# A fused embedding, interaction and MLP kernel: the Gram steps of a group in pairs, and another order for the last group

## The chip, the cores and the metric

The kernel runs on one core of a Trainium2 chip. The metric is the time of one execution on the device in microseconds. A core has five engines with queues of their own: TensorE (PE in the profile; its weight loads are shown apart as PEld), VectorE (DVE), ScalarE (ACT), GpSimd (POOL) and SyncE (SP), which here only issues DMAs. They wait for one another by semaphores.

## What is computed

A recommendation model's forward pass, for a batch of 2048 samples, in fp32:

```
e_k = tbl_k[ids[:, k]]                      # 26 tables, rows of 128
c   = [dense, e_0, ..., e_25]               # 27 features of 128 for each sample
z   = c_n . c_m for all n < m               # 351 products for each sample
h   = relu([dense, z, dense] @ W_top1 + b_top1)   # 607 -> 512
h   = relu(h @ W_top2 + b_top2)                   # 512 -> 256
y   = h @ W_top3                                  # 256 -> 1
```

## The kernel before

The batch is cut into 8 groups of 256 samples, and a group into 2 tiles of 128. Each group goes through these stages.

- **Looks.** Ten tables have only 1000 rows. They stay in SBUF, split into a high and a low part (`table_high`, `table_low`). VectorE compares ids with row numbers (`matches`, L455) and TensorE multiplies the tables by these 0/1 matrices: `look(g, r)` (L300) is 16 matmuls of 256 columns. ScalarE copies the result, transposed, into the tile `turned` (`take_look`, L498). There are two `match` buffers, so the match of a look may be written once the look two before it has ended.
- **Gathers and turns.** The other 16 tables are gathered by POOL with indirect DMAs, 128 rows each, four tables at a time (L284 to L293). `turn(g, k)` (L315) transposes four such blocks on TensorE, 4 matmuls. A group has 8 turns: turns 0 to 3 for its first tile, 4 to 7 for its second. `take_turned` (L504) copies each into `turned`.
- **Gram steps.** `gram(g, k)` (L325) multiplies, for a quarter of the group's samples, the 27 features of each by themselves. In the profile one step is 128 small matmuls (32 columns of weights, 27 moving), each with a weight load of its own. A group has 4 steps. `take_gram` (L516) copies a step's result into the tile `grams`.
- **Repack.** SP writes `grams` to a scratch buffer in HBM and reads it back into `pairs`, in the layout that layer 1 wants (`repack`, L209). It waits for the copy of the last Gram step.
- **Layers.** `layer1(g, o)` (L344) for o = 0 to 3 is 8 matmuls each, `layer2` (L361) 16, `layer3` (L369) 4; ScalarE applies bias and relu (`relu1`, `relu2`) and copies y.

Turns and Gram steps share three PSUM buffers, `mid_ps`. They are numbered in the order in which TensorE issues them (`turn_number`, L168; `gram_number`, L176); an item uses buffer number % 3 and waits until the item three before it has been copied out:

```
after(pe, mid_out, number - 2)
```

The order of all this is written out by hand, once for TensorE (L376 to L451) and once, to match, for ScalarE (L543 to L620). In the period of group g (L391 on), TensorE runs the Gram steps of group g-1, turns of group g, looks of groups g and g+1, and the layers of group g-2:

```
gram(g-1,0) turn(g,0) look(g,6) layer1(g-2,0) layer1(g-2,1)
gram(g-1,1) turn(g,1) look(g,7) layer1(g-2,2) layer1(g-2,3)
gram(g-1,2) turn(g,2) look(g,8) layer2(g-2)
gram(g-1,3) turn(g,3) look(g,9) layer3(g-2)
turn(g,4) look(g+1,0) look(g+1,1) turn(g,5) look(g+1,2)
turn(g,6) look(g+1,3) turn(g,7) look(g+1,4) look(g+1,5)
```

The last group has an order of its own (L428 to L451), in which its own four Gram steps follow too, before the layers of the groups 6 and 7. SP's queue is also in a fixed order (L255 to L271): ids for later looks, the repack, the store of y.

Of the kernel before, what the change touches and what calls it, by code (L numbers as in the profile page):

```python
# [15 lines left out]
AHEAD = 6  # L16
# [6 lines left out]
TURNS = TILES * UNITS  # L23
# [20 lines left out]
def build(nc, dense_t, index_t, look_rows_t, tables, w1_dense, w1_pairs, b1, w2, b2, w3, y):  # L44
# [11 lines left out]
    with ctx:  # L56
# [104 lines left out]
            return 2 * number + 2  # L161

        PERIOD = TURNS + STEPS

        def turn_number(g, k):  # L168
            if g == 0:
                return k  # L170
            first = TURNS + PERIOD * (g - 1)
            if k >= STEPS and g + 1 == groups:
                return first + (10, 11, 12, 13)[k - STEPS]
            return first + (2 * k + 1 if k < STEPS else k + STEPS)

        def gram_number(g, k):  # L176
            first = TURNS + PERIOD * g
            if g + 1 == groups:
                return first - PERIOD + (8, 9, 14, 15)[k]
            return first + 2 * k  # L180

        block = ctx.enter_context(nc.Block())

# [115 lines left out]
        def _(pe):  # L299
            def look(g, r):  # L300
                number, pair = look_number(g, r), pair_number(g, r // 2)
                if g == 0:
                    pe.wait_ge(tables_split, r + 1)

                after(pe, looked, pair - 1)
                pe.wait_ge(match_ready, number + 1)
                for c in range(PARTS):
                    for part in (table_high, table_low):
                        last = nc.tensor.matmul(look_ps[pair % 2][:, r % 2, :], part[0:table_rows, r, c, :],  # L309
                                                match[number % 2][0:table_rows, c, :],  # L310
                                                start=(c == 0 and part is table_high),
                                                stop=(c == PARTS - 1 and part is table_low))
                last.then_inc(look_done, 1)

            def turn(g, k):  # L315
                j, u = g * TILES + k // UNITS, k % UNITS
                number = turn_number(g, k)
                after(pe, mid_out, number - 2)
                pe.wait_ge(gathered[j % 2][u], 16 * UNIT_OF * (j // 2 + 1))
                for n in range(UNIT_OF):  # L320
                    last = nc.tensor.transpose(mid_ps[number % 3][:, n * P:(n + 1) * P],  # L321
                                               rows[j % 2][:, u * UNIT_OF + n, :], identity[:])
                last.then_inc(turn_done, 1)

            def gram(g, k):  # L325
                number = gram_number(g, k)
                if k == 0:

                    pe.wait_ge(mid_out, turn_number(g, TURNS - 1 if g + 1 < groups else UNITS - 1) + 1)
                    pe.wait_ge(looked, pair_number(g, LOOK_PAIRS - 1) + 1)  # L330
                    pe.wait_ge(dense_put, g + 1)
                if k == STEPS // TILES and g + 1 == groups:
                    pe.wait_ge(mid_out, turn_number(g, TURNS - 1) + 1)
                after(pe, mid_out, number - 2)
                for i in range(IN_STEP):
                    for s in range(QUADS):
                        x = k * IN_STEP + i
                        n = (x // BLOCK * P + s * BLOCK + x % BLOCK) * FEATURES
                        last = nc.tensor.matmul(  # L339
                            mid_ps[number % 3][s * ROW:(s + 1) * ROW, i * FEATURES:(i + 1) * FEATURES],  # L340
                            turned[g % 2][:, n:n + ROW], turned[g % 2][:, n:n + FEATURES], start=True, stop=True)
                last.then_inc(gram_done, 1)
# [18 lines left out]
            def layer2(g):  # L361
                pe.wait_ge(hidden1_ready, L1 * (g + 1))
                for o in range(L2):
                    for c in range(L1):
                        last = nc.tensor.matmul(layer_ps[0][:, o, :], w2_sb[:, c, o * P:(o + 1) * P], hidden1[:, c, :],  # L365
                                                start=(c == 0), stop=(c == L1 - 1))
                last.then_inc(layer2_done, 1)

            def layer3(g):  # L369
                pe.wait_ge(hidden2_ready, L2 * (g + 1))  # L370
                for c in range(L2):
                    last = nc.tensor.matmul(layer_ps[1][0:1, 0, :], w3_sb[:, c:c + 1], hidden2[:, c, :],  # L372
                                            start=(c == 0), stop=(c == L2 - 1))
                last.then_inc(layer3_done, 1)
# [16 lines left out]
            for g in range(1, groups - 1):  # L391
                if g == 2:
                    pe.wait_ge(weights_summed, 1)
                    pe.wait_ge(weights_in, WEIGHT_DMAS)
                gram(g - 1, 0)
                turn(g, 0)
                look(g, 6)
                if g >= 2:
                    layer1(g - 2, 0)
                    layer1(g - 2, 1)  # L400
                gram(g - 1, 1)
                turn(g, 1)
                look(g, 7)
                if g >= 2:
                    layer1(g - 2, 2)
                    layer1(g - 2, 3)
                gram(g - 1, 2)
                turn(g, 2)
                look(g, 8)
                if g >= 2:  # L410
                    layer2(g - 2)
                gram(g - 1, 3)
                turn(g, 3)
                look(g, 9)
                if g >= 2:
                    layer3(g - 2)
                turn(g, 4)
                look(g + 1, 0)
                look(g + 1, 1)
                turn(g, 5)  # L420
                look(g + 1, 2)
                turn(g, 6)
                look(g + 1, 3)
                turn(g, 7)
                look(g + 1, 4)
                look(g + 1, 5)

            g = groups - 1  # L428
            for k in range(STEPS):
                gram(g - 1, k)  # L430
                turn(g, k)
                look(g, AHEAD + k)
            layer1(g - 2, 0)
            layer1(g - 2, 1)
            gram(g, 0)
            layer1(g - 2, 2)
            gram(g, 1)
            turn(g, 4)
            turn(g, 5)
            turn(g, 6)  # L440
            turn(g, 7)
            layer1(g - 2, 3)
            gram(g, 2)
            layer2(g - 2)
            gram(g, 3)
            layer3(g - 2)
            for g in (groups - 2, groups - 1):
                for o in range(L1):
                    layer1(g, o)
# [42 lines left out]
        def _(act):  # L492
# [71 lines left out]
            act.wait_ge(weights_in, WEIGHT_DMAS)  # L564
            for g in range(1, groups - 1):
                take_gram(g - 1, 0)
                take_turned(g, 0)
                if g >= 2:
                    relu1(g - 2, 0)
                take_gram(g - 1, 1)  # L570
                take_turned(g, 1)
                take_look(g, 3)
                if g >= 2:
                    relu1(g - 2, 1)
                take_gram(g - 1, 2)
                take_turned(g, 2)
                if g >= 2:
                    relu2(g - 2)
                take_gram(g - 1, 3)
                take_turned(g, 3)  # L580
                take_look(g, 4)
                if g >= 2:
                    copy_y(g - 2)
                take_turned(g, 4)
                take_look(g + 1, 0)
                take_turned(g, 5)
                put_dense(g)
                take_turned(g, 6)
                take_look(g + 1, 1)
                take_turned(g, 7)  # L590
                take_look(g + 1, 2)
            g = groups - 1
            take_gram(g - 1, 0)
            take_turned(g, 0)
            take_gram(g - 1, 1)
            take_turned(g, 1)
            take_look(g, 3)
            take_gram(g - 1, 2)
            take_turned(g, 2)
            put_dense(g)  # L600
            take_gram(g - 1, 3)
            take_turned(g, 3)
            take_look(g, 4)
            relu1(g - 2, 0)
            take_gram(g, 0)
            take_gram(g, 1)
            take_turned(g, 4)
            take_turned(g, 5)
            take_turned(g, 6)
            take_turned(g, 7)  # L610
            relu1(g - 2, 1)
            take_gram(g, 2)
            relu2(g - 2)
            take_gram(g, 3)
            copy_y(g - 2)
            for g in (groups - 2, groups - 1):
                for half in range(2):
                    relu1(g, half)
# [51 lines left out]
```

## Time and profile before

| | us |
|---|---|
| median of 3 runs | 382.88 (381.33 to 383.34) |
| the profiled execution | 384.91 |
| its span, first to last instruction | 382.8 |
| PE busy, matmuls | 341.9 (89%) |
| PE busy, weight loads | 304.2 (79%) |
| POOL busy | 252.1 (66%) |
| DVE busy | 193.2 (50%) |
| ACT busy | 125.5 (33%) |

The profile shows one execution. Matmuls overlap, so a matmul's duration is longer than its share of the time; the distance from one start to the next tells what it costs. "Idle before" is the time for which an engine did nothing in front of an instruction, and "<-" names what ended it; "issue" stands where the profile shows nothing that was waited for. The mean clock granted to TensorE was 0.991 of 2.4 GHz.

### The profile page before, as it was taken

The numbers are of one execution on the slowest core, as the hardware profiler recorded it, in microseconds if no ns is written. First come the engines' busy times: TensorE is split into PE (matmuls) and PEld (weight loads), VectorE is DVE, ScalarE is ACT, GpSimd is POOL, SyncE is SP. The second block draws the span as 40 slices with busy tenths as digits, with TensorE's granted clock in tenths as the row PEclk, the third lists the DMA queues.
The fourth block names the chain that finished last, engine by engine and source line by source line (L and its number), as shares of the span: only waits on it lengthen the run. The fifth ranks groups of instructions, "written<-read, shape, count | busy, mean of one in ns | idle before, by whom it ended". The sixth has DMA issues, their size and how long they took to land.

```text
span 382.8 us, 13108 instructions
## 1 busy us (share of the span) xinstructions
PE 341.9 (89%) x6048; PEld 304.2 (79%) x6048; DVE 193.2 (50%) x94; ACT 125.5 (33%) x211; POOL 252.1 (66%) x267
## 2 busy tenths in 40 slices
PE   0788878984999999999999999999999999999995
PEld 0687767883898898898988898889988898977763
DVE  2899996565424396228833495238742595100000
ACT  2235433332132341334322342323322333343122
POOL 3777887777777777777777777777777777500200
PEclk9999999999799999999999999999999999999999
DMA  8975698254322537225632536234622533420400
GB/s 205 222 210 166 170 301 250 58 195 126 126 80 58 193 82 200 58 80 177 149 119 58 194 92 190 58 120 140 187 79 58 193 89 86 144 73 27 154 13 0
DMA packets 30868, 49.57 MB, mean 129 GB/s; under 512 B 17499, under 2 KB 17635, under 8 KB 30686
## 3 DMA queue, kind: packets, MB, share of 16 engines
q1 hardware_dynamic: 22350, 31.68, 27.0%
q0 software_dynamic: 8320, 16.92, 16.8%
q8 instruction: 48, 0.79, 0.9%
q10 hardware_dynamic: 144, 0.13, 0.1%
q14 instruction: 6, 0.05, 0.0%
HBM read 38.21 MB, written 10.49 MB: 127 GB/s over the span
## 4 chain that ended last, share of the span: by engine, by line
PE 72%; POOL 14%; issue 6%; DMA 4%; DVE 2%; ACT 1%; DVEq 0%
PE look_ps L309 28%; POOL rows L290 14%; PE mid_ps L339 13%; PE layer_ps L356 11%; PE layer_ps L365 7%; PE mid_ps L321 7%; PE layer_ps L353 4%; DMA rows<-in_table,index 3%; DVE match L463 2%; PE layer_ps L372 2%; DMA index<-in_index 1%; ACT hidden L528 0%; ACT hidden L534 0%; ACT turned L501 0%; ACT turned L512 0%
## 5 line engine op out<-in xcount | busy, mean ns | idle before, releaser
L290 POOL DMA_INDIRECT rows<-in_table,index x256 | 248.8, 972 | 82.3 <-issue 75.0
L463 DVE TENSOR_TENSOR match<-look_ids,row_number_ps 125x2048 fp32r<-125x2048 int32 x80 | 181.7, 2286 | 132.2 <-PE look_ps L309 122.3
L309 PE MATMUL look_ps<-match,table_high 125*128 125x256 f32 x640 | 165.7, 296 | 20.2 <-DVE table_low L471 18.1
L309 PE MATMUL look_ps<-match,table_low 125*128 125x256 f32 x640 | 159.4, 286 | 0.1
L309 PEld LDWEIGHTS look_ps<-match,table_high 125*128 125x128 f32 x640 | 124.8, 195 | 25.0 <-issue 16.0
L309 PEld LDWEIGHTS look_ps<-match,table_low 125*128 125x128 f32 x640 | 125.1, 195 | 0.0
L339 PEld LDWEIGHTS mid_ps<-turned 128*32 128x32 f32 x4096 | 45.3, 109 | 19.1 <-issue 15.3
L339 PE MATMUL mid_ps<-turned 128*32 128x27 f32 x4096 | 54.4, 195 | 5.5 <-issue 1.7
L501 ACT COPY turned<-look_ps 128x512 f32<-128x512 f32 x40 | 31.9, 798 | 73.5 <-PE look_ps L309 72.2
L508 ACT COPY turned<-mid_ps 128x512 f32<-128x512 f32 x64 | 42.8, 672 | 19.7 <-PE mid_ps L321 19.5
L321 PE MATMUL mid_ps<-identity,rows 128*128 128x128 f32 x256 | 40.6, 283 | 9.4 <-DMA rows<-in_table,index 8.5
L356 PE MATMUL layer_ps<-pairs,w_pairs_sb 117*128 117x256 f32 x192 | 46.7, 378 | 0.0
L356 PEld LDWEIGHTS layer_ps<-pairs,w_pairs_sb 117*128 117x128 f32 x192 | 36.3, 189 | 5.2
L321 PEld LDWEIGHTS mid_ps<-identity,rows 128*128 128x128 f32 x256 | 28.4, 142 | 14.0 <-issue 13.0
L521 ACT COPY grams<-mid_ps 128x432 f32<-128x432 f32 x32 | 16.6, 519 | 49.2 <-PE mid_ps L339 49.2
L365 PE MATMUL layer_ps<-hidden,w_sb 128*128 128x256 f32 x128 | 29.3, 381 | 1.9 <-ACT hidden L528 1.9
L528 ACT ACTIVATE hidden<-layer_ps,b_sb 128x256 f32<-128x256 f32 x32 | 13.4, 470 | 51.3 <-PE layer_ps L356 51.3
L365 PEld LDWEIGHTS layer_ps<-hidden,w_sb 128*128 128x128 f32 x128 | 23.7, 190 | 5.6 <-ACT hidden L528 2.7
L189 POOL DMA_DIRECT2D pairs<-scratch x4 | 2.5, 639 | 26.7 <-DMA scratch<-grams 26.7
L353 PE MATMUL layer_ps<-dense,w_dense_sum 128*128 128x256 f32 x64 | 19.4, 384 | 0.0
L534 ACT ACTIVATE hidden<-layer_ps,b_sb 128x256 f32<-128x256 f32 x16 | 6.7, 470 | 33.6 <-PE layer_ps L365 33.6
L353 PEld LDWEIGHTS layer_ps<-dense,w_dense_sum 128*128 128x128 f32 x64 | 11.1, 191 | 1.8 <-issue 0.4
(21 smaller groups left out, 44.8 us busy)
## 6 DMA issues: line engine op xcount, KB each, us to landing
look_ids<-in_look_rows SPq DMA_DIRECT2D x40, 256.0 KB, 4.4
scratch<-grams SPq DMA_DIRECT2D x8, 864.0 KB, 4.4
rows<-in_table,index POOLq DMA_INDIRECT x256
scratch<-grams SPq DMA_DIRECT2D x8, 416.0 KB, 5.2
pairs<-scratch SPq DMA_DIRECT2D x92, 29.2 KB
grams<-in_table SPq DMA_DIRECT2D x4, 448.0 KB
pairs<-in_table SPq DMA_DIRECT2D x3, 448.0 KB
hidden<-in_table SPq DMA_DIRECT2D x3, 448.0 KB
```

The costliest lines, as they stand in the source:

```text
L290: pool.indirect_dma_start(out=rows[j % 2][:, at, :], out_offset=None, in_=tables[GATHERED[at]], in_offset=bass.IndirectOffsetOnAxis(ap=ind ...
L309: last = nc.tensor.matmul(look_ps[pair % 2][:, r % 2, :], part[0:table_rows, r, c, :], match[number % 2][0:table_rows, c, :], start=(c == ...
L321: last = nc.tensor.transpose(mid_ps[number % 3][:, n * P:(n + 1) * P], rows[j % 2][:, u * UNIT_OF + n, :], identity[:])
L339: last = nc.tensor.matmul(mid_ps[number % 3][s * ROW:(s + 1) * ROW, i * FEATURES:(i + 1) * FEATURES], turned[g % 2][:, n:n + ROW], turned[ ...
L353: nc.tensor.matmul(layer_ps[o // 2][:, o % 2, :], w1_dense_sum[:, o * P:(o + 1) * P], dense[:, g * N:(g + 1) * N], start=True, stop=False)
L356: last = nc.tensor.matmul(layer_ps[o // 2][:, o % 2, :], w1_pairs_sb[0:CHUNK_ROWS, c, o * P:(o + 1) * P], pairs[0:CHUNK_ROWS, g % 2, c, :] ...
L365: last = nc.tensor.matmul(layer_ps[0][:, o, :], w2_sb[:, c, o * P:(o + 1) * P], hidden1[:, c, :], start=(c == 0), stop=(c == L1 - 1))
L463: nc.vector.tensor_tensor(match[number % 2][0:table_rows], look_ids[b][0:table_rows, r % 2].unsqueeze(1).broadcast_to(shape), row_number_p ...
L501: nc.scalar.copy(by_sample[g % 2][:, :, 1 + 2 * pair:3 + 2 * pair], look_ps[number % 2][:].rearrange("d f n -> d n f")).then_inc(looked, 1)
L508: nc.scalar.copy(by_sample[g % 2][:, tile * P:(tile + 1) * P, first:first + UNIT_OF], mid_ps[turn_number(g, k) % 3][:].rearrange("d (f x) ...
L521: nc.scalar.copy(grams[:, :, k * IN_STEP:(k + 1) * IN_STEP], mid_ps[gram_number(g, k) % 3][:, 0:IN_STEP * FEATURES].rearrange("p (x j) -> ...
L528: nc.scalar.activation(hidden1[:, o, :], layer_ps[half][:, o % 2, :], ACT.Relu, bias=b1_sb[:, o:o + 1]).then_inc(hidden1_ready, 1)
```

## The change

In the period of each group, the Gram steps 0 and 1 of the group before stand together in front of turn 0, and the steps 2 and 3 together behind the second half of layer 1. In the last group the same pairs are made, with turns and looks two by two between them; behind them come all four parts of layer 1 of group 5, then the last group's steps 0 and 1 as a pair, layer 2 of group 5, the turns 4 to 7, layer 3, and the steps 2 and 3 as a pair. ScalarE's order follows. The numbers of turns and Gram steps, which give the PSUM buffer and the count to wait for, are now taken from a generator that lists them in the order of issue. No instruction of the computation is added or removed.

```diff
-        PERIOD = TURNS + STEPS
+        def mid_order():
+            yield from (("turn", 0, k) for k in range(TURNS))
+            for g in range(1, groups):
+                for k in (0, 2):
+                    yield from (("gram", g - 1, k), ("gram", g - 1, k + 1), ("turn", g, k), ("turn", g, k + 1))
+                if g + 1 < groups:
+                    yield from (("turn", g, k) for k in range(STEPS, TURNS))
+
+            yield from (("gram", g, 0), ("gram", g, 1))
+            yield from (("turn", g, k) for k in range(STEPS, TURNS))
+            yield from (("gram", g, 2), ("gram", g, 3))
+
+        mid_place = {step: number for number, step in enumerate(mid_order())}
...
@@ TensorE, groups 1 to 6
                 gram(g - 1, 0)
+                gram(g - 1, 1)
                 turn(g, 0)
                 look(g, 6)
                 if g >= 2:
                     layer1(g - 2, 0)
                     layer1(g - 2, 1)
-                gram(g - 1, 1)
                 turn(g, 1)
                 look(g, 7)
                 if g >= 2:
                     layer1(g - 2, 2)
                     layer1(g - 2, 3)
                 gram(g - 1, 2)
+                gram(g - 1, 3)
                 turn(g, 2)
                 look(g, 8)
                 if g >= 2:
                     layer2(g - 2)
-                gram(g - 1, 3)
                 turn(g, 3)
@@ TensorE, group 7
-            for k in range(STEPS):
+            for k in (0, 2):
                 gram(g - 1, k)
+                gram(g - 1, k + 1)
                 turn(g, k)
                 look(g, AHEAD + k)
+                turn(g, k + 1)
+                look(g, AHEAD + k + 1)
             layer1(g - 2, 0)
             layer1(g - 2, 1)
+            layer1(g - 2, 2)
+            layer1(g - 2, 3)
             gram(g, 0)
-            layer1(g - 2, 2)
             gram(g, 1)
-            turn(g, 4)
-            turn(g, 5)
-            turn(g, 6)
-            turn(g, 7)
-            layer1(g - 2, 3)
+            layer2(g - 2)
+            for k in range(STEPS, TURNS):
+                turn(g, k)
+            layer3(g - 2)
             gram(g, 2)
-            layer2(g - 2)
             gram(g, 3)
-            layer3(g - 2)
```

## Rows read from the trace of the kernel before

**Rows 1.** The page, busy time of each engine.
```profile
PE 341.9 (89%) x6048; PEld 304.2 (79%) x6048; DVE 193.2 (50%) x94; ACT 125.5 (33%) x211; POOL 252.1 (66%) x267
```

**Rows 2.** All waits: engine, tile and line, releaser, us in total, times, longest.
```profile
PEld mid_ps L339 <- issue: 15.3, 53, 1.8
```

**Rows 3.** Timeline of PE: start us, us, what, count, idle before.
```profile
96.35 1.09 PE L321 MATMUL mid_ps<-identity,rows 128*128 128x128 f32 x4 [4.26 <-DMA rows<-in_table,index]
```

**Rows 4.** Table of stretches: length, busy time (instructions), granted clock, DMA share, GB/s.
```profile
187.57:229.93 42.36, 41.68 (x758) 37.42 (x757) 22.68 (x11) 14.20 (x25) 32.00 (x35) 1.00 0.44 126
```

**Rows 5.** Table of stretches, L339 alone: Gram steps, start to the next operation's start.
```profile
195.32:197.21 1.89, 1.73 (x128) 1.00 0.22 54
210.83:212.33 1.50, 1.44 (x128) 1.00 0.24 63
336.41:337.63 1.22, 1.22 (x128) 1.00 0.05 13
...
sum 7.96, PE 7.04; mean PE 1.76
```

**Rows 6.** The page, DMA queues: packets, MB, share of 16 engines.
```profile
q8 instruction: 48, 0.79, 0.9%
```

**Rows 7.** Timeline of PE, last group.
```profile
314.99 1.72 PE L339 MATMUL mid_ps<-turned 128*32 128x27 f32 x116
317.00 0.32 PE L339 MATMUL mid_ps<-turned 128*32 128x27 f32 x12 [0.30 <-issue]
...
319.75 1.25 PE L339 MATMUL mid_ps<-turned 128*32 128x27 f32 x95
321.20 0.47 PE L339 MATMUL mid_ps<-turned 128*32 128x27 f32 x33 [0.20 <-issue]
...
324.10 1.06 PE L339 MATMUL mid_ps<-turned 128*32 128x27 f32 x74
325.40 0.90 PE L339 MATMUL mid_ps<-turned 128*32 128x27 f32 x54 [0.24 <-issue]
...
339.56 1.73 PE L339 MATMUL mid_ps<-turned 128*32 128x27 f32 x128
...
342.74 1.31 PE L321 MATMUL mid_ps<-identity,rows 128*128 128x128 f32 x10 [0.65 <-issue]
...
347.35 0.38 PE L339 MATMUL mid_ps<-turned 128*32 128x27 f32 x20 [0.30 <-issue]
```

**Rows 8.** DMA queues: the stretches 314.7 to 315.7, 318.5 to 319.9, 192.8 to 194.
```profile
q8 instruction: 1, 0.02, 5.5%
...
q8 instruction: 1, 0.02, 5.7%
...
q8 instruction: 1, 0.02, 4.6%
```

**Rows 9.** Table of stretches, all engines, as rows 4.
```profile
189.00:193.00 4.00, 4.00 (x73) 3.83 (x61) 1.93 (x2) 1.09 (x2) 2.91 (x4) 1.00 0.97 279
```

**Rows 10.** Timeline of PE, from a look into a Gram step.
```profile
187.24 0.28 PE L309 MATMUL look_ps<-match,table_high 125*128 125x256 f32 x1
187.36 0.28 PE L309 MATMUL look_ps<-match,table_low 125*128 125x256 f32 x1
187.57 0.62 PE L339 MATMUL mid_ps<-turned 128*32 128x27 f32 x49
```

**Rows 11.** Table of stretches, PE: a turn behind a Gram step, one behind a look.
```profile
189.35:189.77 0.42, 0.42 (x11) 1.00 0.82 307
180.52:180.88 0.36, 0.36 (x6) 1.00 0.09 22
```

**Rows 12.** Timeline of ACT, the last three copies of turned rows.
```profile
343.22 1.74 ACT L508 COPY turned<-mid_ps 128x512 f32<-128x512 f32 x3 [0.65 <-PE mid_ps L321]
```

**Rows 13.** Timeline of SP, the last repack's reads.
```profile
358.87 6.26 SPq L189 DMA_DIRECT2D pairs<-scratch  x8
```

**Rows 14.** Table of stretches, all engines, behind the wait of rows 3.
```profile
96.30:101.00 4.70, 4.65 (x22) 4.68 (x23) 0.04 (x1) 0.67 (x1) 3.48 (x5) 0.50 0.46 149
```

More of the change, by code:

```diff
@@ L161, in pair_end @@
             return 2 * number + 2
-        PERIOD = TURNS + STEPS
-        def turn_number(g, k):
[L169 to L174, printed above, removed]
+        def mid_order():
[9 more added lines that the diff above has]
+        mid_place = {step: number for number, step in enumerate(mid_order())}
+        def turn_number(g, k):
+            return mid_place["turn", g, k]
         def gram_number(g, k):
[L177 to L180, printed above, removed]
+            return mid_place["gram", g, k]
         block = ctx.enter_context(nc.Block())
@@ L566, in _ @@
                 take_gram(g - 1, 0)
+                take_gram(g - 1, 1)
                 take_turned(g, 0)
@@ L569, in _ @@
                     relu1(g - 2, 0)
-                take_gram(g - 1, 1)
                 take_turned(g, 1)
@@ L575, in _ @@
                 take_gram(g - 1, 2)
+                take_gram(g - 1, 3)
                 take_turned(g, 2)
@@ L578, in _ @@
                     relu2(g - 2)
-                take_gram(g - 1, 3)
                 take_turned(g, 3)
@@ L593, in _ @@
             take_gram(g - 1, 0)
+            take_gram(g - 1, 1)
             take_turned(g, 0)
-            take_gram(g - 1, 1)
             take_turned(g, 1)
@@ L598, in _ @@
             take_gram(g - 1, 2)
+            take_gram(g - 1, 3)
             take_turned(g, 2)
             put_dense(g)
-            take_gram(g - 1, 3)
             take_turned(g, 3)
@@ L604, in _ @@
             relu1(g - 2, 0)
+            relu1(g - 2, 1)
             take_gram(g, 0)
             take_gram(g, 1)
[L607 to L611, printed above, removed]
+            relu2(g - 2)
+            for k in range(STEPS, TURNS):
+                take_turned(g, k)
+            copy_y(g - 2)
             take_gram(g, 2)
-            relu2(g - 2)
             take_gram(g, 3)
-            copy_y(g - 2)
             for g in (groups - 2, groups - 1):
```

## The prediction, made before the changed kernel was run

> **What bounds the kernel now.** I read the page's engine table first: TensorE is busy 341.9 of 382.8 us, the next engine (POOL) 252.1 [rows 1]. Then the waits, of which the weight loads of the Gram steps hold 15.3 us with no engine named, only "issue" [rows 2]. PE's long idle stretches are in the opening; the last, 4.26 us for gathered rows, ends at 96.35, when the last block of rows of group 1 lands [rows 3]. Up to there the gathers set the pace. From 102.92 on, one group follows another, five of them alike; the one shown takes 42.36 us with PE busy for 41.68, in 758 matmuls [rows 4]. VectorE works 22.7 and ScalarE 14.2 us of it, so what is added to or taken from PE's own stream between 103 us and the end moves the end one for one. The change reorders that stream, so the question is what an order costs PE.
>
> **A limit that busy shares hide: PE's instruction supply.** A Gram step is 128 matmuls and 128 weight loads in 1.50 to 1.89 us [rows 5], while a look has 16 of each in 2.0 us. The table of queues has a queue "instruction" with 48 packets and 0.79 MB, 16.4 KB each [rows 6]; PE has 2 x 6048 instructions [rows 1] and some waits, 12,288 being 48 x 256. So PE's program comes in blocks of 256. Now read the pauses "<-issue" in the last group [rows 7]: the first Gram step pauses after 116 matmuls, the next after 95, the next after 74. From pause to pause that is 12 + 4 (a turn) + 16 (a look) + 95 = 127, and 33 + 4 + 16 + 74 = 127 matmuls: 254 instructions and two waits, 256 each time. Go on counting and you reach the middle of turn 5 (pause at 342.74) and matmul 108 of a later Gram step (pause at 347.35), both there in the rows. PE stops at borders of blocks.
>
> How fast can blocks follow? The block's packet lies in 314.7 to 315.7 and PE goes on at 317.00; in 318.5 to 319.9 and it goes on at 321.20 [rows 7, 8]. So the packet of the next block starts only after the border before it has been passed (317.00, then a packet after 318.5), one block is on its way at a time, and it is usable some 1.4 us after its packet. From border to border, where PE had to wait for it: 4.20 us twice, 4.6 (342.74 to 347.35), and 3.1 (the border 7 matmuls into the step at 339.56, to 342.74) [rows 7]. I call this turnaround R and take R = 4.0, bounds 3.1 and 4.6. Where other transfers are heavy it can be worse: after the border some 1.5 us into the step of 187.57, the packet is found only in 192.8 to 194 [rows 8], with the DMA engines 97% busy before it [rows 9]. That makes 192.9 + 0.9 + 1.4 - 189.1 = 6.1 us, which hurts nobody today, since 256 slow instructions follow.
>
> This is why order matters. At 1.75 us per 256 instructions a Gram step eats a block in less than half of R. Today each step is followed by 40 to 72 slow instructions, and the border in the next step is mostly reached after R is over.
>
> **The change, part by part.**
> *Steps 0 and 1 together (groups 2 to 6).* A period has 4 x 256 + 10 x 32 + 8 x 8 + 64 + 32 + 8 = 1512 instructions and about 20 waits, 1532 = 6 x 256 - 4: the borders wander by 4 instructions per group. In the last group the first lies 232 into the first step [rows 7], so in groups 2 to 6 it lies 212 to 228 into it. With one step after the other, the second border is 256 Gram instructions later, always inside the pair. It is due after 1.75 us and open after R: PE stands 4.0 - 1.75 = 2.25 us. Bounds: 1.35 (R 3.1), 4.35 (R 6.1; the ids' transfers that fill the DMA engines there are partly gated by the matches, so they stay near).
> *Steps 2 and 3 together.* The pair starts 664 instructions after the first one, so its borders lie at 60 to 76 and 316 to 332. Layer 1 in front is slow (108 ns per instruction, 3.46 us for 32) and lets instructions be queued ahead; I assume the first border is passed about 0.4 us before the pair starts. DMA is quiet around today's steps 1 and 3 (22 and 24% against 97% [rows 5, 9]), so R = 3.6: open at 3.2, due at 322 / 256 x 1.75 = 2.2, cost 1.0. Bounds 0.5 and 2.0 (R 3.1 and 4.6).
> *What goes.* Two entries and two exits of Gram steps per group. A step begins 0.21 us after a look's last matmul, where the next look matmul comes after 0.12 [rows 10], and a turn behind a step takes 0.42 us where it takes 0.36 behind a look [rows 11]; that is 0.15 a step, 0.3 per group.
> Of this the Trainium skill (TensorEngine Tiling (Array Packing), Key Properties) says that changing the tiling mode drains TensorE; the trace agrees, with 0.15 us as the drain's size. Such a rule alone would have this change win.
> Group: 2.25 + 1.0 - 0.3 = 2.95, five groups: 14.8 us.
> *Last group's first four steps.* Between the pairs stand two turns and two looks; the borders are at 228 and 484, then at 144 and 400 of the second pair: twice 2.25. Today the four slots from 314.99 on take 7.96 us, each from its step's start to the next turn's [rows 5], against 4 x 1.75: 1.0 us of waiting is paid already. 4.5 - 1.0 - 0.3 = 3.2.
> *The tail.* Steps 0 and 1 of group 7 have borders at about -3, 253 and 509, steps 2 and 3 at about 175 and 431: twice 2.25 again. What goes is today's wait in turn 5 (0.9 from start to start) and in step 2 (0.5), and 0.3 of entries. Added is a wait for ScalarE: after layer 2 of group 5 come its two relus (some 0.9 us), then four copies of turned rows (three take 1.74 us [rows 12], so 2.3 in all), while PE has the turns (1.7 us) and layer 3 (1.0) for cover in place of 1.8 us of layer 1: 3.2 against 2.7, about 0.5. Sum: 4.5 - 1.4 - 0.3 + 0.5 = 3.3. The last repack stays about hidden: the issues of its pairs run from 358.87 to 365.1 [rows 13], and the last layer 1 begins at some 367 today; layer 3 (0.7 us) no longer stands in that cover, so up to 0.5 more could show, which I keep for the range.
> *At nothing.* Group 1: its pairs cost 3 us too, but PE idles 4.26 us for rows behind them [rows 3], which absorbs it. It could even give something back: after the 4.26 us the granted clock is 0.50 for 4.7 us [rows 14], the lower level, 1.2 GHz; were the idle shorter, up to 2 us come back (not in the sum). ScalarE has the same operations; its copies are due later. Waits on the three turning buffers: each is for an item three back, and the item before a pair's turn is a turn or step that was copied at least a look earlier. SP's queue: the repack waits for step 3, which now stands one turn, one look and layer 2 earlier, hence scratch, pairs and ids move forward together. POOL's gathers wait for turns that come a little later; they run ahead by then.
>
> Sum: 14.8 + 3.2 + 3.3 = 21.3 us on the profiled execution's 384.91 us, 406.2. That execution is 2.0 us above the median of 382.88 (0.5%), so as a median: **404.2 us**.
>
> **Rivals.**
> A, *the supply keeps up* (381, faster): if two blocks or more were kept ahead, the pairs would cost nothing and only 0.3 us for each of seven stretches go: -2.1, with 0.5 back for the tail, so 381.3. It decides at the pair's second border: stall or none. For it: the weight loads of the steps pause 53 times, but 15.3 us in all [rows 2], and in groups 2 to 6 PE is nearly never idle. Against it: the 256 count and the constant lag behind the packet.
> The Trainium skill (Runtime: NRT & Kernel Launch, Instruction fetch mechanics) gives TensorE room for 2048 instructions, and by that a pair of 512 would never stall and rival A would hold; the same section also speaks of only two lines of 256. The trace sides with the second: 4.2 us per block when blocked.
> B, *even* (383): the short pauses inside steps, about 0.5 us of each slot (1.50 to 1.89 against 1.22 for the step at 336.41 [rows 5]), are not repeated in a pair's second step and pay for much of the stall. It needs R below 2.3, under every interval read.
> C, *the clock falls too* (432): idle of 2 us in 14 pairs lowers the granted clock as it did after 4.26 us; each time 4.7 us at half clock would cost about 2 us: 28 more. Against it: pauses of 0.65 us (0.9 from start to start) are followed by none that the table of slots shows [rows 5], and 2.2 us is nearer to these than to 4.26.
>
> **Numbers.** Forecast 0.80, A 0.10, B 0.05, C 0.05. All terms at their low bounds: 1.55 x 5 + 1.4 + 1.0 = 10.2, with 2 back from the clock 8.2, 391; all high: 6.05 x 5 + 5.9 + 4.5 = 40.6, 423.5. The terms will not all sit at one end, so 391 to 416 leaves out A, B, C and the far end. About 0.5% can be told from no change: faster 0.09, same 0.06, slower 0.85.
>
> **What would show it.** Groups of about 45.3 us in place of 42.4. Gram pairs of 5.5 to 6 us (first) and 4.3 to 5 (second), with one pause "<-issue" of 1 to 2.5 us in each, 256 instructions after another border and 1.4 us behind an instruction packet. The opening to 96.35 unchanged. I am wrong if pairs take 3.5 us and the pauses don't grow; half wrong if the second pair shows none.

## The result, and the profile after

| | before | changed |
|---|---|---|
| median of 5 runs, us | 382.88 (380.83 to 383.71) | 426.52 (420.87 to 427.94) |
| ratio | | 1.110, 95% interval 1.103 to 1.117 |
| profiled execution, us | 384.91 | 420.87 |
| its span, us | 382.8 | 418.8 |
| granted clock, mean | 0.991 | 0.950 |

The changed kernel is 11% slower. The forecast was slower, 404.2 us, with a range that ended at 416. The ratio leaves out the two slowest runs of the changed kernel (427.26 and 427.94 us), which are over 1.5% above its fastest. The profiled execution is the fastest of the five; in the others the mean granted clock was 0.943 to 0.955, and the 5.6 us between it and the median have no trace of their own.

First the page of the changed kernel, busy times and the queue of instruction blocks. PE's busy time grew by 10 us, its span by 36; the blocks are the same 48.

```profile
PE 351.9 (84%) x6048; PEld 316.5 (76%) x6048; DVE 193.2 (46%) x94; ACT 126.2 (30%) x211; POOL 252.9 (60%) x267
...
q8 instruction: 48, 0.79, 0.8%
```

Then the waits of the changed kernel (engine, tile, line <- releaser: us in total, times, longest). The weight loads of the Gram steps [rows 2] went from 15.3 to 40.9 us of "issue" in the same 53 pauses, and the matmuls now show 29.8 us of their own. (These two overlap; the step's line is L341 here.)

```profile
PEld mid_ps L341 <- issue: 40.9, 53, 3.4
...
PE mid_ps L341 <- issue: 29.8, 19, 3.3
...
PEld mid_ps L341 <- ACT turned L511: 0.5, 1, 0.5
```

The last line is the wait for ScalarE in front of the last pair, which the prediction put at about 0.5 us.

The table of stretches for the groups 2 to 6, for the last group up to layer 1 of group 6, and for the rest (columns as in rows 4). What took 42.36 us [rows 4] takes 46.8 to 50.1, and the granted clock is no longer 1.00.

```profile
102.51:149.33 46.82, 43.47 (x758) 39.24 (x757) 23.05 (x11) 14.41 (x25) 35.54 (x38) 0.96 0.43 117
149.33:197.36 48.03, 43.22 (x757) 38.92 (x757) 22.69 (x11) 14.28 (x25) 36.14 (x40) 0.96 0.42 117
...
292.65:342.73 50.08, 42.79 (x758) 39.09 (x757) 22.68 (x11) 14.40 (x25) 30.28 (x33) 0.93 0.34 91
342.73:387.98 45.25, 35.99 (x1174) 31.77 (x1173) 6.95 (x4) 14.38 (x26) 6.49 (x7) 0.95 0.17 52
387.98:418.80 30.82, 25.11 (x109) 19.32 (x104) 0.00 (x0) 6.28 (x15) 2.49 (x4) 0.94 0.16 55
```

The same table for the pairs of the groups 2 to 6 alone (columns as in rows 5; three of ten and the sum). The ten pairs take 55.3 us; the twenty steps of before sum up to 34.7, the second fence.

```profile
102.51:107.31 4.80, 3.41 (x256) 1.00 0.38 82
119.08:124.38 5.30, 3.65 (x256) 1.00 0.23 56
...
292.65:301.27 8.62, 3.58 (x256) 0.84 0.42 105
...
sum 55.32, PE 33.63; mean PE 3.36
```

```profile
sum 34.74, PE 32.71; mean PE 1.64
```

So the 36 us of the span go as follows. Groups 2 to 6: 240.2 - 212.1 = 28.2, of which 20.6 inside the pairs and 7.6 outside them. Last group up to layer 1 of group 6: 45.25 against 38.35 (314.99 to 353.34), 6.9. The rest 1.3, the opening -0.4.

The pauses stand where instructions were counted to. This is the timeline of PE in the changed kernel: both pairs of group 6, one of group 7.

```profile
292.65 1.58 PE L341 MATMUL mid_ps<-turned 128*32 128x27 f32 x114
295.81 1.79 PE L341 MATMUL mid_ps<-turned 128*32 128x27 f32 x128 [1.59 <-issue]
300.91 0.43 PE L341 MATMUL mid_ps<-turned 128*32 128x27 f32 x14 [3.31 <-issue]
...
314.85 1.65 PE L341 MATMUL mid_ps<-turned 128*32 128x27 f32 x168
318.44 0.95 PE L341 MATMUL mid_ps<-turned 128*32 128x27 f32 x88 [1.94 <-issue]
...
383.56 1.78 PE L341 MATMUL mid_ps<-turned 128*32 128x27 f32 x128 [1.85 <-issue]
387.29 0.75 PE L341 MATMUL mid_ps<-turned 128*32 128x27 f32 x40 [1.95 <-issue]
```

Borders after 114 and 242 matmuls are instructions 228 and 484; after 168, instruction 336. In between lie exactly 128 matmuls and their loads. From border to border it takes 5.10 us in the first pair shown and 3.73 in the last.

Each pause ends behind the packet of a block. The first pair of the last group pauses until 347.86; the second line shows the DMA queues of the stretch 345.2 to 346.5, with its packet:

```profile
347.86 0.32 PE L341 MATMUL mid_ps<-turned 128*32 128x27 f32 x12 [1.59 <-issue]
...
q8 instruction: 1, 0.02, 5.9%
```

In this trace all 18 pauses at borders from 102 us on end 1.3 to 1.6 us after such a packet has ended. How soon the packet starts varies more. Behind the border of 151.71 it starts after 1.2 us, behind that of 295.81 only after 2.6. The queue q1, which carries the ids, tells the difference. The first line is the stretch 151.71 to 152.88, the second 295.81 to 298.38, where a broadcast of 144 packets comes before the block's packet:

```profile
q1 hardware_dynamic: 2, 0.00, 2.6%
...
q1 hardware_dynamic: 144, 0.26, 48.2%
```

What lies outside the pairs is the clock, nearly all of it in the looks: TensorE is busy for 114.0 us with the looks of the groups 2 to 6, where it was 106.5 before. Behind the pause of 3.31 us the looks come every 0.21 us in place of 0.12, and the table of stretches (all engines, last-but-two column the clock) has it at the lower of its two levels, 1.2 GHz, for nearly 7 us (298.5 to 305.35), then back at 2.4:

```profile
298.00:305.40 7.40, 4.49 (x34) 4.43 (x35) 0.00 (x0) 1.19 (x2) 4.25 (x5) 0.54 0.19 48
305.40:312.00 6.60, 6.60 (x42) 6.03 (x42) 2.79 (x2) 1.90 (x4) 3.49 (x4) 1.00 0.17 39
```

### The profile page after: what moved, and what is told of

Same layout as the page of the kernel before. It is cut to its first block, busy times and chain, and to the rows that moved or that the text cites. A ratio compares the mean times of both kernels' runs of the same rounds, so it can differ in the third digit from the quotient of the medians.

```text
span 418.8 us, 13108 instructions
## 1 busy us (share of the span) xinstructions
PE 351.9 (84%) x6048; PEld 316.5 (76%) x6048; DVE 193.2 (46%) x94; ACT 126.2 (30%) x211; POOL 252.9 (60%) x267
## 4 chain that ended last, share of the span: by engine, by line
PE 65%; POOL 16%; issue 13%; DVE 3%; DMA 2%; ACT 1%; DVEq 0%
PE look_ps L311 26%; POOL rows L292 16%; PE mid_ps L341 11%; PE layer_ps L358 10%; PE layer_ps L367 7%; PE mid_ps L323 5%; PE layer_ps L355 4%; DVE match L466 3%; PE layer_ps L374 2%; DMA index<-in_index 1%; DMA rows<-in_table,index 1%; ACT hidden L537 0%; ACT hidden L531 0%; ACT turned L511 0%; ACT y_row L544 0%
## 5 line engine op out<-in xcount | busy, mean ns | idle before, releaser
L311 PE MATMUL look_ps<-match,table_high 125*128 125x256 f32 x640 | 173.3, 305 | 18.9 <-DVE table_low L474 16.8
L311 PE MATMUL look_ps<-match,table_low 125*128 125x256 f32 x640 | 166.4, 295 | 0.5 <-issue 0.5
L311 PEld LDWEIGHTS look_ps<-match,table_high 125*128 125x128 f32 x640 | 130.6, 204 | 24.4 <-issue 15.6
L311 PEld LDWEIGHTS look_ps<-match,table_low 125*128 125x128 f32 x640 | 130.9, 205 | 0.0
L341 PE MATMUL mid_ps<-turned 128*32 128x27 f32 x4096 | 55.2, 198 | 33.6 <-issue 29.8
L341 PEld LDWEIGHTS mid_ps<-turned 128*32 128x32 f32 x4096 | 46.6, 112 | 44.3 <-issue 40.9
L323 PEld LDWEIGHTS mid_ps<-identity,rows 128*128 128x128 f32 x256 | 30.2, 145 | 12.7 <-issue 10.6
L191 POOL DMA_DIRECT2D pairs<-scratch x4 | 2.5, 640 | 43.6 <-DMA scratch<-grams 43.6
```

Source lines behind the costliest of these rows:

```text
L341: last = nc.tensor.matmul(mid_ps[number % 3][s * ROW:(s + 1) * ROW, i * FEATURES:(i + 1) * FEATURES], turned[g % 2][:, n:n + ROW], turned[ ...
```

## The experiments

**e1 and e2: the two parts of the change, each alone.** e1 has pairs in the groups 1 to 6 and the last group of before; e2 has it the other way round.

```diff
# e1: TensorE's and ScalarE's last group, and the numbering, are those of before
-            for k in (0, 2):
+            for k in range(STEPS):
                 gram(g - 1, k)
-                gram(g - 1, k + 1)
                 turn(g, k)
...
# e2: the groups 1 to 6 are those of before
                 gram(g - 1, 0)
-                gram(g - 1, 1)
                 turn(g, 0)
```

> Only the groups 1 to 6 have their Gram steps in pairs; the last group is in the order of before. Theory S (instruction supply: TensorE's program arrives in blocks of 256 instructions, one on its way at a time, so a pair of 512 waits 1.5 to 3.5 us at a border, and long pauses lower the clock): the five periods from 102 us on grow from 42.4 to about 48 us as in the changed kernel, some 28 us, so about 411 to 418 us. Rival T (the last group's new order is what costs, through ScalarE's copies and the last repack): about 385.

> Only the last group has the new order; the groups 1 to 6 are in the order of before. Theory S: the four pairs of the last group pause as in the changed kernel (1.8, 2.3, 1.5, and 2.1 with 2.2 us), the stretch from its first Gram step to layer 1 of group 6 grows by about 7 us and the end by 1 us of slower clock: 389 to 392. Rival T: over 410. The two parts should add up: e1 and e2 together give about 40 us.

Measured: e1 406.01, 407.84, 419.29 and 419.61 us, e2 392.72 (390.02 to 394.58; ratio 1.023, 1.016 to 1.030), beside 383.14 for before. e1's runs lie in two pairs, 12 us apart. Their median, 413.57, is in the range of theory S, but no single run is. So the sum of the medians' differences, 30.4 + 9.6 = 40.0, agrees with the forecast of 40 by luck: with e1's two quicker runs, 406.9, it is 33.4. The two profiled executions are firmer. In e1 the groups 2 to 6 grew from 212.1 to 241.2 us, by 29.1 where some 28 were expected; the opening was 4.9 us and the end 2.9 us shorter than before, so that the span grew by 21.3. In e2, which ends 0.7 above its range, the stretch from the last group's first Gram step to layer 1 of group 6 grew from 38.35 to 48.35 us, by 10.0 where 7 were expected, at a mean clock of 0.92:

```profile
313.55:361.90 48.35, 39.48 (x1174) 0.92 0.22 66
```

Rival T wanted 385 for e1 and over 410 for e2; it falls. The table of stretches of e1's groups 2 to 6 separates the pauses from the clock:

```profile
97.98:144.04 46.06, 42.44 (x757) 1.00 0.45 124
144.04:191.52 47.48, 43.66 (x758) 0.96 0.41 117
191.52:237.65 46.13, 42.42 (x757) 1.00 0.41 119
237.65:287.28 49.63, 43.15 (x758) 0.93 0.40 110
287.28:339.15 51.87, 45.11 (x757) 0.87 0.32 88
```

In two groups the clock stayed at 1.00: they take 46.06 and 46.13 against 42.19 and 42.36 before, so the pauses alone cost 3.8 us a group. Where the clock was at 0.93 or 0.87 a group takes 49.6 and 51.9. A group also has longer pauses there, so not all of that is the clock's.

**e3 and e4: half of the instructions.** The same two orders, with wider matmuls. e3 is made from the changed kernel, e4 from the one before.

```diff
-                for i in range(IN_STEP):
+                for i in range(0, IN_STEP, 2):
...
-                            mid_ps[number % 3][s * ROW:(s + 1) * ROW, i * FEATURES:(i + 1) * FEATURES],
-                            turned[g % 2][:, n:n + ROW], turned[g % 2][:, n:n + FEATURES], start=True, stop=True)
+                            mid_ps[number % 3][s * ROW:(s + 1) * ROW, i * FEATURES:(i + 2) * FEATURES],
+                            turned[g % 2][:, n:n + ROW], turned[g % 2][:, n:n + 2 * FEATURES], start=True, stop=True)
```

> The changed order, but each Gram step is 64 matmuls of 54 columns in place of 128 of 27: half of the instructions for the same columns (the products of the second sample of each two are not the right ones; copies, PSUM buffers and all else are the same). Theory S: a pair is 256 instructions, has one border and no long pause; pairs take 2.5 to 3.2 us, and the kernel is within 1% of e4, about 370 to 378 us (the gathers need some 40 us a group and become the bound). Rival A2 (two steps in a row stall for the array's or PSUM's sake, not for the number of instructions): pauses of 1 to 3 us remain in the pairs, and it is 25 us or more slower than e4.

> The order of before with the same half-count Gram steps as e3. Theory S: the steps drop from 1.75 to about 1.3 us, with hardly a pause inside; 370 to 378 us. Rival A2: the same here, since it differs only for pairs.

Measured: e3 369.69 us (367.83 to 370.73), e4 375.98 (375.27 to 376.64). Pairs of 256 instructions are not slower than single steps; here they are faster by 6.3 us, more than the 1% expected. The table of stretches for pairs of e3 (L341; the third is one of the two that still paused), then for steps of e4 (L339):

```profile
181.50:183.52 2.02, 2.02 (x128) 1.00 0.35 109
195.29:197.27 1.98, 1.98 (x128) 1.00 0.15 41
220.69:224.15 3.46, 2.00 (x128) 1.00 0.35 101
```

```profile
180.87:181.84 0.97, 0.97 (x64) 1.00 0.66 202
187.81:188.84 1.03, 1.03 (x64) 1.00 0.12 32
```

A pair is 2.0 us (2.5 to 3.2 were expected), two single steps are 2.0 us. Whole groups without a wait for rows or a long pause, each from its first Gram step to the next group's, are compared in the tables of e3 and of e4:

```profile
142.28:181.50 39.22, 38.91 (x502) 1.00 0.44 127
181.50:220.69 39.19, 38.88 (x502) 1.00 0.44 130
```

```profile
141.57:180.87 39.30, 38.99 (x502) 1.00 0.43 127
180.87:220.24 39.37, 39.06 (x502) 1.00 0.43 130
```

Two steps in a row cost nothing for the array's or PSUM's sake: rival A2 falls. The pairs save some 0.1 us a group, so the 6.3 us are not the saved entries. In the profiled executions they are the opening (e3's group 2 starts at 99.02, e4's at 102.28) and the stretch from the last group's first step on, 65.9 against 74.3 us, with shorter waits for gathered rows; the groups 2 to 6 as a whole take 202.5 in e3 and 196.6 in e4, since e3 has in them a wait for rows, a stretch at the lower clock behind it, and two pauses of 1.5 and 0.8 us. Where TensorE waits for nothing else, then, the order of the change costs nothing with half of the instructions, and 3.8 us or more a group with all of them. The width of the matmuls changed with their number; that the number is what counts follows from this together with the counted places of the pauses, the packets in front of their ends, and e5.

**e5: the borders moved, the work left alone.**

```diff
             pe.wait_ge(pads_zeroed, 2)
+            for _ in range(48):
+                nc.tensor.matmul(layer_ps[0][0:ROW, 0, 0:FEATURES], identity[:, 0:ROW], identity[:, 0:FEATURES],
+                                 start=True, stop=True)
```

> The changed kernel with 48 small matmuls (192 instructions, results unused) put into TensorE's idle opening, so that every later border of 256 instructions comes 192 instructions earlier in the work. Theory S: in the groups 2 to 6 the pauses move: in the first pair from matmul 108 and 236 to about 12 and 140, in the second from 160 to about 66 and 194. The first pair gains from instructions queued ahead (its pause at 140 under 1.5 us), the second pays fully (1.5 to 2.3). The sum stays near: 415 to 428. Rival W (a pause belongs to a place in the work, such as a PSUM buffer, a wait or the ids' transfers): pauses stay at 108 and 236, and 160.

Measured: 416.64 us (414.43 to 417.12), ratio 1.086 (1.080 to 1.093), within the range and some 10 us below the changed kernel (4.6 in the profiled spans). The timeline of PE in e5, first and second pair of group 5:

```profile
241.20 2.10 PE L341 MATMUL mid_ps<-turned 128*32 128x27 f32 x144
244.57 1.42 PE L341 MATMUL mid_ps<-turned 128*32 128x27 f32 x112 [1.27 <-issue]
...
259.67 2.99 PE L341 MATMUL mid_ps<-turned 128*32 128x27 f32 x198
264.14 0.88 PE L341 MATMUL mid_ps<-turned 128*32 128x27 f32 x58 [1.49 <-issue]
```

The pauses of the groups 2 to 6 stand after matmul 138 to 146 and 192 to 200, where counting puts them. In the changed kernel they stood at 108 to 114 with 234 to 242, and at 160 to 168. The pauses moved with the count of instructions and not with the work: rival W falls. With the first border at 12 matmuls the first pair has only one pause, under 1.5 us as expected; in the second pairs the pauses are 1.1 to 2.8 us, where 1.5 to 2.3 were expected.

**e7: less traffic beside the blocks.**

```diff
+                if number >= 3 * LOOK_PAIRS:
+                    sp.dma_start(look_ids[b][0:1].rearrange("p r n -> p (r n)"),
+                                 look_rows_t[number:number + 1, :]).then_inc(look_ids_in[b], 16)
+                    return
```

> The changed kernel, but from group 3 on the 256 KB broadcasts of ids are replaced by 2 KB transfers to one partition (so the matches there compare stale ids). It tests whether the transfers set how long a block takes. If so, in the groups 4 to 6 the first pair's pauses fall from 2.0 to 3.5 us to about 1.5, its first border has none, the rest is the same, and the kernel takes 405 to 415. If the turnaround has nothing to do with the traffic: pauses as before, and 420 or more.

Measured: 416.92 us (413.07 to 420.99), ratio 1.082 (1.074 to 1.090), between the two expectations. First pairs of groups 5 and 6 in the tables of e7 and of e1, which has the same pairs and the full transfers (the changed kernel's are 5.96 and 8.62):

```profile
241.22:246.80 5.58, 3.98 (x258) 1.00 0.20 52
286.77:292.61 5.84, 3.46 (x258) 0.99 0.24 59
```

```profile
237.65:246.06 8.41, 3.51 (x257) 0.80 0.40 100
287.28:295.70 8.42, 3.90 (x258) 0.69 0.43 106
```

The pairs of over 8 us are gone. They are the three, one in the changed kernel and two in e1, in which a broadcast of 144 packets came between a border and the next block's packet: that packet started 2.4 to 2.8 us behind the border and the pause grew to 2.8 to 3.5 us. In e7 it starts 1.1 to 1.6 us behind the borders inside the first pairs, and no pause of the groups 4 to 6 is over 2.2. So traffic on the queues can hold a block up by more than 1 us. The rest of what was expected did not come: the first border still pauses in two of the three groups, and the pair of group 4 is 6.56 us long, where the changed kernel's is 5.20. Over the groups 3 to 6 the first pairs are 2.8 us shorter than in the changed kernel, about as much as the profiled span (416.1 against 418.8); the 10 us between the medians are not explained by that.

**e9: pauses without the instruction supply.** In the order of before, TensorE waits for ScalarE twice a group.

```diff
+                pe.wait_ge(mid_out, gram_number(g - 1, 1) + 1)
...
+                pe.wait_ge(mid_out, gram_number(g - 1, 3) + 1)
...
+                if k in (1, 3) and g < groups - 2:
+                    for b in range(2):
+                        after(act, spare_done, 2 * (2 * g + k // 2) + b)
+                        nc.scalar.copy(spare[:], mid_ps[gram_number(g, k) % 3][:, 0:IN_STEP * FEATURES]).then_inc(
+                            spare_done, 1)
```

> The order of before, with pauses made another way: in the groups 1 to 6 TensorE waits, behind Gram step 1 and behind step 3, until ScalarE has copied that step's result, and ScalarE copies it two times more into a spare tile first. Same TensorE instructions and borders. Each pause is three copies of 0.52 us and their latencies, about 1.8 us, ten of them behind 102 us: 18 to 20 us of pure waiting, so 401 to 403 if TensorE's clock does not mind. Theory C (pauses of 1.5 to 2 us lower the granted clock now and then, whatever makes them): stretches at the lower level stand in the record after some of the pauses, the looks behind them take 3 in place of 2 us, and the kernel takes 403 to 412. Rival (only pauses of the instruction supply go with the lower clock): the clock stays at full speed from 102 us on and the time is 401 to 403.

Measured: 407.49 us (405.26 to 410.11), ratio 1.063 (1.060 to 1.067), in the range of theory C. The wait of e9, and its table for PE, once around a pause and once behind it:

```profile
PE mid_ps L323 <- ACT grams L530: 21.5, 12, 1.9
```

```profile
154.96:158.67 3.71, 1.73 (x129) 0.97 0.21 52
158.67:162.51 3.84, 3.84 (x20) 0.58 0.21 57
```

Twelve waits of 1.8 us, ten of them behind the opening, are 18 us; 25 were measured. Behind the first wait shown, a turn and a look take 3.84 us at a clock of 0.58, where rows 11 and a look of 2.0 us make 2.4. So the clock can fall around a pause of under 2 us, whoever makes it. Behind 102 us there are six such stretches; five begin inside one of these waits or up to 1.4 us behind it, the sixth behind a long "issue" pause. Not all of the other 7 us is the clock: PE's own "issue" pauses in Gram steps are also longer in e9, 6.3 us in all against 1.7 before, one of 2.8 us among them.

**e6 and e8: the other direction.** Half steps, in front of the turn and behind the look; e6 everywhere, e8 with the last group of before.

```diff
-                gram(g - 1, 0)
+                gram(g - 1, 0, 0)
                 turn(g, 0)
                 look(g, 6)
+                gram(g - 1, 0, 1)
```

> The other way: from the kernel before, each Gram step is cut into halves of 64 matmuls, one in front of the turn and one behind the look, in the groups 1 to 6; in the last group as far as there is work to put between. Same instructions. Theory S: no long pause, and the short pauses inside steps (0.5 us of each 1.75 us slot) shrink, since 128 instructions at a time are queued better; against that stand 0.15 us for each of 32 more entries, 5 us. From 373 (pauses gone) to 386 (none gone). Rival M (what counts is the change of the tiling mode, not the supply): 388 or more, and the changed kernel would have had to be faster.

> Half steps as in e6 in the groups 1 to 6, the last group in the order of before. In e6 the groups 2 to 6 took 41.8 us each in place of 42.4 to 42.6, but its last group lost about 4 us. Theory S: the gain stays and the loss goes: 378.5 to 381 against 382.8, ratio 0.990 to 0.996. Rival: the two are within the noise, ratio 0.998 to 1.002.

Measured: e6 383.66 us, ratio 1.002 (0.999 to 1.004); e8 381.24, ratio 0.998 (0.995 to 1.000). Most half steps in e6 take 0.69 us, with no pause (table for L342):

```profile
234.08:234.77 0.69, 0.69 (x64) 1.00 0.57 154
237.25:237.95 0.70, 0.69 (x64) 1.00 0.07 18
```

Two such are 1.38 where a step was 1.50 to 1.89 [rows 5]; the eight of group 5 take 5.9 us together, where a group's four steps took 6.9. The groups took 41.8 us, 0.6 less. Four more entries at 0.15 us would cost 0.6 of the 1.0 saved inside the steps, and 0.4 are missing; that was not tested by itself. In the last group of e6 the steps 2 and 3 stand too near each other and pause by 1.2 us. e6 is in its range, and rival M (388 or more) falls with it. e8's ratio lies in the range of its rival, no gain: it is 0.2% below before, by its interval up to 0.5%. None of the orders tried is clearly faster than that of before.

## Why the prediction was wrong

The mechanism of the pauses was right, and the sum, 21.3 us, was half of the 43.6 measured. The step that failed is the clock: the prediction put the lower clock at nothing in the sum and gave it, as rival C, a chance of 0.05 of its own. The profiled execution grew by 36.0 us, 14.7 more than the sum. Of these, 8.9 are time at the lower clock, 7.6 outside the pairs of the groups 2 to 6 and 1.3 at the end, and 5.8 lie inside the pairs of these groups (20.6 against 14.8). The 7.6 us by which the median grew more than the profiled execution have no trace, and their cause stays open.

- *The limit.* Blocks of 256, one on its way, usable about 1.4 us behind the packet: e3 and e5 confirm the first part, the 18 packets, each of which ends 1.3 to 1.6 us before a pause does, the rest. The positions came out to within 4 instructions (468 to 484 forecast and found for the second border of the first pair, 316 to 332 forecast and 320 to 336 found in the second pair, 175 and 431 forecast and 176 and 432 found in the last).
- *The pairs of groups 2 to 6.* The forecast of 5.75 and 4.5 us makes 51.3 for ten; they took 55.3. The turnaround was near what was taken (counted back from the pauses, 3.1 to 4.0 us mostly), with two misses. Only the second border of the first pair was charged; in three of five groups the first one paused too (0.88, 0.26 and 1.59 us), since the border before it lay just ahead of the pair. And where ids were transferred a turnaround reached 5.1, behind the border of 295.81. Of the 0.3 us a group that would be saved, e3 and e4 show some 0.1. Pauses alone: 3.8 us a group in e1, against 2.95.
- *The clock, rival C.* It got 0.05, because pauses of 0.65 us had left it at full speed and 4.26 us had not. The pairs' pauses, most of them 1.2 to 3.3 us, lie between, and behind the opening the clock is at its lower level in seven stretches of 3.4 or 6.8 us. Each begins inside a pair's pause or up to 1.6 us behind it, and before the change there is none from 102 us to the end. Outside the pairs the groups 2 to 6 lost 7.6 us by it, which is nowhere in the sum, and the end 1.3. C as written, a fall in all 14 pairs, was too much; none was too little. e9 shows that a wait of another kind does it as well.
- *Last group and tail.* 3.2 + 3.3 = 6.5 forecast, 6.9 measured, partly by luck. Four pauses of 2.25 us were charged, one for each pair; there were five that make 8.9 in all, 1.59, 2.15 and 1.32 us in the first three pairs, and 1.85 with 1.95 in the last. The wait of 0.5 for ScalarE was there. In e2 the same stretch cost 10.0, its clock being lower as well. The 0.5 us that the prediction kept for the range of the tail is missing in its upper sum, 4.5.
- *Group 1 at nothing.* Right: the opening ended 0.4 us earlier.
- *Rival A* (the supply keeps up) is out, as pauses of up to 3.3 us at the borders show. With it goes the room for 2048 instructions of which the Trainium skill speaks (Runtime: NRT & Kernel Launch, Instruction fetch mechanics); its two lines of 256 agree with the trace, in which every pair of 512 instructions has a pause of 1.1 us or more at a border. *Rival B* had a point that did not help it: in three pairs (263.34, 314.85 and 352.94) the short pauses are not there and both steps together take 2.5 us beside the pause at the border, but that pause is then 1.8 to 2.2 us, longer than the 1.2 to 1.6 of pairs with short pauses and one long one. What is saved on the way to the border is waited for at it.
- *The median.* 21.3 us were added to a median, while the profiled execution grew by 36.0 and the median by 43.6. The mean granted clock of the five runs goes from 0.943 to 0.955, and the sum from one trace has no term for such differences.

## What to carry to other kernels

Count instructions, not only time: a stretch of many small matmuls is limited by how fast the engine's program arrives, here 256 instructions per 3.1 to 4.2 us, and up to 5.1 beside other transfers, and slow instructions between such stretches are what hides it. A pause "<-issue" that comes again after the same count of instructions gives it away before any change is made. And when a change adds pauses of 1.5 us and more to a busy TensorE, put some time at the lower clock behind them into the sum.

## What was not expected of the hardware

A wait of 1.8 to 1.9 us went with 3.4 us at 1.2 GHz in some places and with none in others (e9: five such stretches for ten waits behind 102 us; e1: two groups with both pauses and a clock of 1.00). Half as many Gram instructions of twice the width took 0.97 to 1.03 us a step in place of 1.50 to 1.89 (e4). And with all 128 matmuls a step could take 1.22 us [rows 5], so 0.3 to 0.7 us of the others is not needed for the matmuls themselves.
